# Two-layer latent transformer kernel: query work moved ahead, dequantisation shared out differently, and several pieces of work reordered

## The chip, the cores and the metric

The kernel runs on one core of a Trainium2 chip. A core has five engines that run at the same time, each through its own instruction list in order: PE (TensorE, matrix products), DVE (VectorE), ACT (ScalarE), POOL (GpSimd) and SP (SyncE, which here only starts DMA transfers). They meet through semaphores. The metric is the device time of one execution in microseconds (us). PE's clock has two levels in the records, 2.4 GHz (granted clock 1.00) and 1.2 GHz (0.50); a stretch that has both shows a value between.

## The reference

Sixteen samples of 64 latent rows (1024 rows of 512, held as 8 tiles of 128) attend to contexts of 1601 rows of 256. With LN the layer norm and x the latent rows:

```
x = x + cross_attention0(LN(x), ctx)   # 16 heads of 32, projections Wq Wk Wv Wo with biases
x = x + state_space(LN(x))             # 16 heads, 64 states, masked decay matrix, gate, W_out, b_out
x = x + block_ffn(LN(x))               # 16 blocks of 128 hidden units, the best 4 by a router kept
x = x + cross_attention1(LN(x), ctx)   # one head: q = LN(x) Wq + bq, k = ctx Wk + bk, v = ctx Wv + bv
x = x + self_attention(LN(x))          # causal
x = x + quantised_ffn(LN(x))           # weights to 4 bits in groups of 32; activations to 16 bits,
                                       # each with one scale from the largest magnitude of the tensor
```

Weights of the last line are quantised so, with w in groups of 32 along a row:

```
s  = max(max|w| / 7, 1e-12)
wq = clip(round(w / s), -8, 7) * s
```

## The kernel before

The kernel is a chain of stages. Each stage is a block in which every engine has a hand-written instruction list, and all engines wait for each other between two blocks. The stages and their times in the profiled execution are: cross attention 0 (0 to 864.3 us), state space (to 1000.2), block FFN (to 1231.65), queries of cross attention 1 (to 1288.0), its batches (to 1434.8), self attention (to 1491.75) and quantised FFN (to 1747.1). Nothing but the written order decides when an instruction comes; there is no planner.

Precision is kept by splitting: an fp32 operand becomes a bf16 high part and a bf16 rest (low part), and three products are taken. Some stages use fp32 matmuls instead, which stand as two records each in the trace.

**Cross attention 0** (`cross0_batches`). At the start DVE makes the high and low halves of the queries (L835, L837), SP writes the queries to DRAM in another layout (L440) and reads them back (L419). POOL builds `picks`, a matrix that chooses heads, out of a memset and three selections on 128x2048 (L518, L521), SP stores it (`head_picks`, L436), and it is read again only in state space and block FFN. Then 16 samples of 8 head pairs follow: scores, softmax, transposes of the probabilities by DMA (L458, L463), products with the values (L621). `ring_events` deals PE's other work, the projections of the next sample (L588) and the outputs of the last (L639), between the pairs. After the last sample a drain remains: the last products, their sums by DVE (L805), the value bias (`folded`, L650), row sums (L657) and the last output tile (L639, L881). Meanwhile SP loads x again tile by tile (L473, in `X_BEHIND`), and `residual(t)` on DVE adds the finished outputs to it (L796) and takes its statistics (L79).

**State space** (`state_space`). After the projections DVE adds the output bias to all eight tiles of x (L1207), each counted by the semaphore `s_xo`. Then come 32 units (tile, group of heads): ACT exponentiates, DVE multiplies the decay matrix in (L1221) and gates (L1212), PE makes the products (L1105, L1127). POOL and SP use the stage to split the block FFN's weights: POOL first waits for all eight counts of `s_xo`, then takes sixteen pieces (high part L994, low part L996), SP loads each piece and stores its two parts (L1037). SP ends the stage with a wait for the last stores.

**Block FFN** (`block_ffn`). PE makes 32 hidden groups (12 matmuls L1366 and a mask L1371 each); ACT applies relu into `masked`, a ring of two buffers (L1421), and rounds the high part (L1410); POOL takes the low part (L1329). Then PE makes 8 output tiles of 48 matmuls (L1401), and DVE adds each to x (L1526). In the same stage `Dequant` quantises the last layer's weights in 36 pieces of 128x512: SP loads a piece, DVE takes the scales, divides and rounds (L2095, L2097, L2099, L2101, L2104, L2106), POOL multiplies by the scale (L2111), ACT rounds the high part (L2118), DVE takes the low part (L2122), SP turns both parts by DMA (L2068) and stores them (L2074). `front_at` and `turn_at` give the slot of each piece: 16 turns fall to hidden groups, 20 come behind them, three pieces to an output tile.

**Queries of cross attention 1** (`cross1_queries`). Scores of one head need q.k = (x Wq + bq).(c Wk + bk), so the kernel turns Wk onto the query side: qT = Wq'x + bq in 8 groups of 4 fp32 matmuls (L1601), a row bk.qT (L1607), and qk = Wk qT in 4 groups (L1614). SP loads the weights, then the first four samples' contexts (13.1 MB). All is PE work behind a layer norm and transposes (L219).

**Quantised FFN** (`quant_ffn`). PE runs 24 gate groups and 24 up groups of 12 matmuls (L2219), then the down product (L2235). DVE takes largest magnitudes (L2341, L2364, L2398), reduces them over the tile (`peak_of`, L2303), has PE spread them over partitions (`spread`, L2204) and computes scales (`unit`). The scale number 2, of the gated values, is found in front of the last up group: `spread(2)` stands before the last 12 matmuls.

## Time and profile before

| what | us |
|---|---|
| median of 3 runs | 1748.54 |
| lowest and highest | 1747.14, 1748.58 |
| the profiled execution | 1748.78 |
| its span (first to last instruction) | 1747.1 |
| PE busy | 1586.8 (91%) |
| DVE busy | 1179.9 (68%) |
| ACT busy | 889.2 (51%) |
| POOL busy | 770.7 (44%) |

Busy shares are means over stages with different limits. Since the engines meet between stages, the time is the sum of the stages' lengths, and each stage ends with its own slowest engine. Where this is not PE, PE shows a gap with the engine it waited for, and behind a long gap its clock is at the lower level for a while. The rows to look for are therefore PE's gaps, the lower clock behind them, and at a stage's end the engines that waited there for the last one.

### The profile page before, as it was taken

What the parts mean: (1) busy time and instruction counts of PE and PEld (TensorE: products, weight loads), DVE (VectorE), ACT (ScalarE), POOL (GpSimd) and SP (SyncE); (2) the same over time, 40 slices, a digit from 0 to 9 for tenths busy, and PEclk for the clock granted to TensorE, in tenths of its full rate; (3) what the DMA queues carried; (4) which work ended last, traced back from release to release, by engine and by line L of the source; (5) the groups of instructions that cost most, each with busy time, mean ns of one, the idle gap of its engine ahead of it and who ended that gap; (6) DMA issues with size and microseconds to landing.
All of it is one profiled execution on the core that took longest, in us unless ns stands there. A gap on an engine that the chain in (4) does not pass through costs nothing. (4 is left out here: it accounts for less than half of the span.)

```text
span 1747.1 us, 33847 instructions
## 1 busy us (share of the span) xinstructions
PE 1586.8 (91%) x13876; PEld 812.5 (47%) x13876; DVE 1179.9 (68%) x1959; ACT 889.2 (51%) x1184; POOL 770.7 (44%) x384
## 2 busy tenths in 40 slices
PE   6999999999999999999589899799789979799459
PEld 3445555555555555554346463244434444344224
DVE  6688888888888888886555468988422223527881
ACT  1377777778777777776273035411111222327650
POOL 1468888888888878875108516633000000000000
PEclk9999999999999999999699979999899999899879
DMA  4489999999999999999617454567838944000001
GB/s 143 115 162 197 192 189 193 193 191 191 198 191 191 192 193 195 192 174 175 141 50 223 149 217 124 145 157 175 338 128 342 397 160 208 0 1 1 0 0 48
DMA packets 556821, 282.72 MB, mean 162 GB/s; under 512 B 483056, under 2 KB 534768, under 8 KB 553600
## 3 DMA queue, kind: packets, MB, share of 16 engines
q1 hardware_dynamic: 556672, 280.63, 67.7%
q8 instruction: 106, 1.74, 0.4%
q14 instruction: 43, 0.35, 0.1%
HBM read 138.74 MB, written 22.54 MB: 92 GB/s over the span
## 5 line engine op out<-in xcount | busy, mean ns | idle before, releaser
L564 POOL TENSOR_TENSOR x<-x_prob,x 128x1604 bf16<-128x1604 f32 x120 | 387.9, 3233 | 144.7 <-ACT x L720 144.7
L850 DVE TENSOR_REDUCE x_negmax<-x_score 128x1 f32<-128x1604 f32 x128 | 233.6, 1825 | 17.7 <-PE x_score L605 7.4
L588 PE MATMUL x_ring<-x_ctx_hi,wk_split 128*128 128x400 bf16 (+1 forms) x1024 | 218.3, 335 | 4.4 <-DVE x_kT L778 4.4
L710 ACT ACTIVATE x_prob<-x_score,x_negmax 128x1604 f32<-128x1604 f32 x128 | 204.8, 1600 | 25.7 <-DVE x_negmax L850 20.9
L588 PE MATMUL x_ring<-wv_split,x_ctx_hi 128*128 128x512 bf16 (+1 forms) x832 | 214.2, 380 | 0.0
L778 DVE SCALAR_TENSOR_TENSOR x_kT<-x_ring,bk,x_kT 128x400 bf16<-128x400 f32 (+1 forms) x256 | 162.0, 634 | 34.6 <-ACT x_kT L699 26.6
L720 ACT CAST x<-x_prob 128x1604 bf16<-128x1604 f32 x120 | 183.0, 1525 | 0.0
L784 DVE TENSOR_TENSOR x_v<-x_ring,x_v 128x512 bf16<-128x512 f32 (+1 forms) x208 | 143.7, 691 | 52.8 <-ACT x_v L703 50.0
L699 ACT ACTIVATE x_kT<-x_ring,bk 128x400 bf16<-128x400 f32 (+1 forms) x196 | 116.4, 594 | 98.0 <-PE x_ring L588 97.0
L588 PEld LDWEIGHTS x_ring<-x_ctx_hi,wk_split 128*128 128x128 bf16 x1024 | 94.4, 97 | 92.4 <-issue 21.1
L703 ACT CAST x_v<-x_ring 128x512 bf16<-128x512 f32 (+1 forms) x148 | 86.5, 585 | 97.2 <-PE x_ring L588 97.2
L2219 PE MATMUL g_bank<-g_x_split,g_w 128*128 128x512 bf16 x576 | 129.0, 388 | 6.4 <-DVE g_x_split L2335 6.4
L621 PE MATMUL x_pv<-x_pT,x_v 128*64 128x128 bf16 (+1 forms) x3328 | 119.0, 222 | 13.0 <-DMA x_pT<-x_kT 5.7
L588 PE MATMUL x_ring<-x_ctx_lo,wk_split 128*128 128x400 bf16 (+1 forms) x512 | 129.3, 334 | 0.0
L621 PEld LDWEIGHTS x_pv<-x_pT,x_v 128*64 128x64 bf16 (+1 forms) x3328 | 98.2, 111 | 64.2 <-issue 58.7
L588 PEld LDWEIGHTS x_ring<-wv_split,x_ctx_hi 128*128 128x128 bf16 (+1 forms) x832 | 77.4, 99 | 102.3 <-DVE x_kT L778 9.2
L588 PE MATMUL x_ring<-wv_split,x_ctx_lo 128*128 128x512 bf16 (+1 forms) x416 | 123.7, 379 | 0.0
L2196 POOL MEMSET g_round<- 128x1 f32 x1 | 0.1, 98 | 272.5 <-POOLq L1845 272.5
L513 POOL TENSOR_TENSOR x_ctx_lo<-x_stage,x_ctx_hi 128x802 bf16<-128x802 f32 (+1 forms) x64 | 106.1, 1658 | 29.6 <-DVE x_ctx_hi L759 28.3
L1401 PE MATMUL f_bank<-f_w,f_h 128*128 128x512 bf16 x384 | 85.4, 385 | 16.2 <-POOL f_h L1329 13.8
L506 POOL TENSOR_TENSOR x_ctx_hi<-x_stage,x_zero 128x800 bf16<-128x800 f32 (+1 forms) x60 | 91.3, 1521 | 9.6 <-DMA x_stage<-in_ctxT 7.7
L2219 PEld LDWEIGHTS g_bank<-g_x_split,g_w 128*128 128x128 bf16 x576 | 57.5, 100 | 77.2 <-DVE g_x_split L2335 6.6
(332 smaller groups left out, 2491.2 us busy)
## 6 DMA issues: line engine op xcount, KB each, us to landing
y_ctx<-in_ctx SPq DMA_DIRECT2D x16, 1664.0 KB, 10.5
y_ctxT<-in_ctxT SPq DMA_DIRECT2D x16, 1601.0 KB, 13.6
x_stage<-in_ctxT SPq DMA_DIRECT2D x48, 400.0 KB, 4.5
x_q_rows<-q_rows SPq DMA_DIRECT2D x64, 128.0 KB, 3.1
m_xT<-in_L_ffn_w SPq DMA_DIRECT2D x16, 512.0 KB, 4.6
ffn_w_parts<-m_xT SPq DMA_DIRECT2D x32, 256.0 KB, 2.6
x_stage<-in_ctxT SPq DMA_DIRECT2D x16, 401.0 KB, 5.0
f_w<-ffn_w_parts SPq DMA_DIRECT2D x4, 1024.0 KB, 9.1
```

The costliest lines, as they stand in the source:

```text
L506: pool.tensor_tensor(chi[:, :, QW * c:QW * c + n], stage[:, c % 2, :, 0:n], zero[:].unsqueeze(2).broadcast_to([P, KC, n]), ALU.add).then_i ...
L513: pool.tensor_tensor(clo[:, :, at], stage[:, c % 2, :, 0:n], chi[:, :, at], ALU.subtract).then_inc(clo_done, 1)
L564: pool.tensor_tensor(ph[:, g % 2, 1, 0:NKP], prob[:, g % 2, :], ph[:, g % 2, 0, 0:NKP], ALU.subtract).then_inc(pl_done, 1)
L588: last = pe.matmul(out_, lhs, rhs, start=(i == 0), stop=(i == len(steps) - 1))
L621: last = pe.matmul(pv[L * h:L * h + L, 0:2 * L], v[0:kw, vpar, t, 2 * pp + h, :, :].rearrange("p s d -> p (s d)"), pT[0:kw, u, :, t, L * h ...
L699: nc.scalar.activation(kT[:, par, 0, m, n0:n0 + w], ring[g % RING][:, 0:w], ACT.Identity, bias=bk[:, KD * turned(c) + m:KD * turned(c) + m ...
L710: nc.scalar.activation(prob[:, g % 2, :].rearrange("p (c n) -> p c n", n=QW), scores, ACT.Exp, bias=nmax[:, g % 2:g % 2 + 1], accum_out=rs ...
L720: nc.scalar.copy(ph_of[g >= LAST][:, g % 2, 0, 0:NKP], prob[:, g % 2, :]).then_inc(ph_done, 1)
L778: dve.scalar_tensor_tensor(kT[:, par, 1, m, n0:n0 + w], ring[g % RING][:, 0:w], bk[:, KD * turned(c) + m:KD * turned(c) + m + 1], kT[:, pa ...
L784: dve.tensor_tensor(v[0:kw, par, m, :, 1, :], ring[g % RING][0:kw, :].rearrange("p (h d) -> p h d", h=H), v[0:kw, par, m, :, 0, :], ALU.su ...
L850: dve.tensor_reduce(nmax[:, pair % 2:pair % 2 + 1], scores, mybir.AxisListType.XY, ALU.max, negate=True).then_inc(max_done, 1)
L2219: last = pe.matmul(banks[2 + n % NB_G][:], wt[:, hw, j, m * P:(m + 1) * P], xs[:, hx, j, 512 * c:512 * c + 512], start=(i == 0 and j == 0) ...
```

## The change

1. *Start.* On POOL the four memsets of the `ph` padding (L542, which wait for the stored queries) come ahead of `picks` and its three selections; on SP the store of `picks` and the wait for it move behind the store of the queries, their reads, four chunk loads and the load of `Wo`. PE gets 18 matmuls on an identity matrix ahead of its first transposes.
2. *Drain.* The loads of x tiles 6 and 7 move from behind pair 6 of the last sample to behind pair 7, with a semaphore of their own; `residual` is called for tiles (0,1,2), (3), (4) and, after the last output piece, (5,6,7), where it was (0 to 3), (4,5), (6,7). PE gets 20 such matmuls before the last pair's products, 8 before and 8 after the folded bias.
3. *State space.* The eight bias adds move into the unit loop, one behind `mixed(n)` of units 4 to 11.
4. *Block FFN.* The ring `masked` has three buffers. The multiplication by the scale goes from POOL to DVE, the low part from DVE to POOL. Behind the turn of piece 23 SP loads Wq transposed, [Wk transposed | bk] and bq into the space of w1 (1.5 MB), and behind the last output tile PE makes the product Wq.[Wk'|bk] from them (16 fp32 matmuls of 257 columns, 12 of one column); ACT copies it out.
5. *Queries of cross attention 1.* qT is gone: qk comes from x in 4 groups of 4 matmuls with the product, and 8 matmuls make the bias row. Four weight loads are gone, the context loads go sample pair by sample pair, and DVE adds the folded query bias.
6. *Self attention and quantised FFN.* 15 identity matmuls at the start of each; in the latter 18 more behind the transposes and 12 before the down product. Scale 2 is found behind the last up group, the 15 steps of the gate chain are spread over 12 tiles instead of 11, and `AHEAD` goes from 3 to 1.

```diff
+    def keep_busy(self, pe, ident, bank, count):
+        pattern = ident[:].bitcast(BF16)
+        for _ in range(count):
+            pe.matmul(bank[:, 0:2 * P], pattern[:, 0:P], pattern, start=True, stop=True)
...
-        X_BEHIND = {2: (0,), 3: (1, 2), 4: (3,), 5: (4, 5), 6: (6, 7)}
+        X_BEHIND = {2: (0,), 3: (1, 2), 4: (3,), 5: (4, 5), 7: (6, 7)}
+        X_EARLY = 6
...
-            sp.wait_ge(s_pick, 4)
-            sp.dma_start(k.picks, picks.rearrange("p h n -> p (h n)")).then_inc(s_kept, 16)
-            sp.wait_ge(s_kept, 16)
             sp.wait_ge(s_qlo, len(qgroups))
...
             for c in range(4):
                 low_part(0, c)
+            pool.wait_ge(spilled, 64)
+            for u in range(2):
+                for h in range(2):
+                    pool.memset(ph_of[0][:, u, h, NKP:NKT], 0.0).then_inc(set_ph, 1)
             pool.memset(picks, 0.0).then_inc(s_pick, 1)
...
+            pe.wait_ge(norm.s_stats, 5)
+            k.keep_busy(pe, ident, ring[0], 18)
             norm.on_tensor(pe)
...
+                            if e[1] == PAIRS - 1:
+                                pe.wait_ge(exp_done, PAIRS)
+                                k.keep_busy(pe, ident, score[:, 0:512], 20)
                             products(e[1])
...
-                    if b == B and p < 2:
-                        for t in ((0, 1, 2, 3), (4, 5))[p]:
+                    if b == B and p < 3:
+                        for t in ((0, 1, 2), (3,), (4,))[p]:
                             residual(t)
...
-            for t in range(NT):
-                dve.tensor_tensor(x[:, t, :], x[:, t, :], bO[:], ALU.add).then_inc(s_xo, 1)
...
                 mixed(n)
+                if 4 <= n < 4 + NT:
+                    dve.tensor_tensor(x[:, n - 4, :], x[:, n - 4, :], bO[:], ALU.add).then_inc(s_xo, 1)
...
+MASKED = 3
...
+            def late_weights():
+                sp.wait_ge(s_h, len(groups))
+                sp.dma_start(bq[:], d["L1_xattn_bq"]).then_inc(s_late, 16)
+                sp.dma_start(wqT, d["L1_xattn_WqT"].rearrange("(j p) n -> p j n", p=P)).then_inc(s_late, 16)
+                sp.dma_start(wkb, d["L1_xattn_WkTb"].rearrange("(j p) n -> p j n", p=P)).then_inc(s_late, 16)
...
-                for i in dq.fronts(n):
-                    dq.multiply_on_gpsimd(pool, i)
-            for i in range(dq.EARLY, dq.count):
-                dq.multiply_on_gpsimd(pool, i)
+                for i in dq.turns(n):
+                    dq.low_on_gpsimd(pool, i)
...
+            pe.wait_ge(s_late, 48)
+            for a in range(KD):
+                for j in range(KD):
+                    last = pe.matmul(banks[2 + a][:, 0:CD + 1], wqT[:, j, a * P:(a + 1) * P], wkb[:, j, :],
+                                     start=(j == 0), stop=(j == KD - 1))
+                last.then_inc(s_next, 1)
...
-                if n >= 2:
-                    act.wait_ge(s_hlo, n - 1)
+                if n >= MASKED:
+                    act.wait_ge(s_hlo, n - MASKED + 1)
...
-                for i in dq.turns(n):
-                    dq.low_on_vector(dve, i)
...
-                    last = pe.matmul(wide[n % 3][:], wq[:, j, m * P:(m + 1) * P],
+                    last = pe.matmul(keyed[n][:], wqk[:, j, m * P:(m + 1) * P],
                                      xT[:, j, 512 * c:512 * c + 512], start=(j == 0), stop=(j == KD - 1))
...
-        if i >= self.SLOTS:
-            dve.wait_ge(self.s_back, i - self.SLOTS + 1)
...
+        dve.wait_ge(self.s_unit, 6 * i + 6)
+        dve.tensor_tensor(blocks, blocks, s.unsqueeze(2).broadcast_to([P, 512 // QB, QB]),
+                          ALU.mult).then_inc(self.s_back, 1)
...
-                if n == half + 2 * FIRST:
-                    spread(2)
+            spread(2)
             spread(3)
             spread(4)
+            k.keep_busy(pe, ident, banks[1], 12)
```

At the start of the kernel, POOL's list around `picks` (named x_pT here, the padding x 128x60) reads before:

```order
L518 MEMSET x_pT 128x2048
L521 AFFINE_SELECT x_pT<-x_pT 128x2048 x3
L523 MEMSET tri 128x128
L524 MEMSET low 128x128
L527 AFFINE_SELECT tri<-tri 128x128
L531 AFFINE_SELECT tri<-tri 128x64
L534 AFFINE_SELECT low<-low 128x128
L537 AFFINE_SELECT low<-low 128x64
L542 MEMSET x 128x60 x4
```

and now:

```order
L529 MEMSET x 128x60 x4
L530 MEMSET x_pT 128x2048
L533 AFFINE_SELECT x_pT<-x_pT 128x2048 x3
L535 MEMSET tri 128x128
L536 MEMSET low 128x128
L539 AFFINE_SELECT tri<-tri 128x128
```

The padding, which waits for the stored queries, now stands ahead of all of them.

In state space, DVE's list between the gate projections (m_gT) and the units reads before (m_bO is the output bias):

```order
L1204 TENSOR_SCALAR m_gT<-m_banks,m_bG 128x512 x8
L1207 TENSOR_TENSOR x<-x,m_bO 128x512 x8
L1221 TENSOR_TENSOR m_mix<-m_decay,m_banks 128x2x128 x6
L1212 TENSOR_TENSOR m_xhat<-m_banks,m_gT 128x128
L1221 TENSOR_TENSOR m_mix<-m_decay,m_banks 128x2x128 x2
L1212 TENSOR_TENSOR m_xhat<-m_banks,m_gT 128x128
```

and now:

```order
L1221 TENSOR_SCALAR m_gT<-m_banks,m_bG 128x512 x8
L1236 TENSOR_TENSOR m_mix<-m_decay,m_banks 128x2x128 x6
L1227 TENSOR_TENSOR m_xhat<-m_banks,m_gT 128x128
L1236 TENSOR_TENSOR m_mix<-m_decay,m_banks 128x2x128 x2
L1227 TENSOR_TENSOR m_xhat<-m_banks,m_gT 128x128
L1236 TENSOR_TENSOR m_mix<-m_decay,m_banks 128x2x128 x2
L1246 TENSOR_TENSOR x<-x,m_bO 128x512
L1227 TENSOR_TENSOR m_xhat<-m_banks,m_gT 128x128
L1236 TENSOR_TENSOR m_mix<-m_decay,m_banks 128x2x128 x2
L1246 TENSOR_TENSOR x<-x,m_bO 128x512
```

One add stands behind each unit from the fifth on, so the eighth count of `s_xo` comes with the twelfth unit.

From the block FFN's output tiles (f_h) to the first scores of cross attention 1, PE's list reads before:

```order
L1401 MATMUL f_bank<-f_w,f_h 128x512 x384
L1254 UNCONDITIONAL_BRANCH
L1589 UNCONDITIONAL_BRANCH
L219 MATMUL yq_bank<-ident,yq_xhat 128x128 x32
L1601 MATMUL yq_bank<-yq_xT,yq_wq 128x512 x32
L1607 MATMUL yq_bank<-yq_qT,yq_bk 1x512 x8
L1614 MATMUL yq_bank<-yq_qT,yq_wkT 128x512 x16
```

and now:

```order
L1436 MATMUL f_bank<-f_w,f_h 128x512 x384
L1442 MATMUL f_bank<-f_w 128x257 x16
L1447 MATMUL f_bank<-f_next_bq,f_w 128x1 x8
L1450 MATMUL f_bank<-f_next_bq,f_w 1x1 x4
L1274 UNCONDITIONAL_BRANCH
L1628 UNCONDITIONAL_BRANCH
L225 MATMUL yq_bank<-ident,yq_xhat 128x128 x32
L1635 MATMUL yq_bank<-yq_xT,wqk 128x512 x12
L1641 MATMUL yq_bank<-yq_xT,wqk 1x512 x8
L1635 MATMUL yq_bank<-yq_xT,wqk 128x512 x4
```

The 32 matmuls of the query projection are gone from the second stage, and 28 small ones have come to the end of the first (an empty branch marks the passage between stages).

## Rows read from the trace of the kernel before

**Rows 1.** Timeline of DVE, start: start us, us, line, op, out<-in, [idle before <-releaser]

```profile
44.20 0.69 DVE L837 TENSOR_TENSOR x<-x_prob,x 128x512 bf16<-128x512 f32 x1
...
49.17 2.39 DVE L837 TENSOR_TENSOR x<-x_prob,x 128x512 bf16<-128x512 f32 x1
```

**Rows 2.** Timeline of POOL, start

```profile
49.01 6.56 POOL L521 TENSOR_SCALAR_AFFINE_SELECT x_pT<-x_pT 128x2048 bf16<-128x2048 bf16 x3
```

**Rows 3.** Timeline of PE, start

```profile
56.96 1.52 PE L588 MATMUL x_ring<-x_ctx_hi,wk_split 128*128 128x401 bf16 x4 [4.12 <-DVE x_kT L778]
```

**Rows 4.** Stretch: us, busy of PE PEld DVE ACT POOL, PEclk, DMA share, GB/s

```profile
56.00:62.00 6.00, 5.04 (x16) 2.29 (x17) 2.71 (x9) 1.19 (x2) 0.99 (x4) 0.50 0.67 189
```

**Rows 5.** Timeline of PE, drain of cross attention 0

```profile
833.44 3.70 PE L639 MATMUL x_ring<-wo,catT 128*128 128x512 f32 x8
...
843.47 1.59 PE L621 MATMUL x_pv<-x_pT,x_v 128*64 128x128 bf16 x26 [5.48 <-DMA x_pT<-x_kT]
850.36 1.60 PE L621 MATMUL x_pv<-x_pT,x_v 128*64 128x128 bf16 x26 [5.29 <-DVE x_kT L805]
...
856.34 6.11 PE L639 MATMUL x_ring<-wo,catT 128*128 128x512 f32 x8 [1.01 <-DVE catT L866]
```

**Rows 6.** Timeline of DVE in state space

```profile
910.79 4.89 DVE L1207 TENSOR_TENSOR x<-x,m_bO 128x512 f32<-128x512 f32 x8
...
919.34 0.75 DVE L1221 TENSOR_TENSOR m_mix<-m_decay,m_banks 128x256 f32<-128x256 f32 x2 [0.81 <-PE m_banks L1127]
```

**Rows 7.** Timeline of PE in state space

```profile
916.40 0.43 PE L1105 MATMUL m_banks<-m_mix,m_xn 128*32 128x128 f32 x8 [1.79 <-DVE m_mix L1221]
```

**Rows 8.** Timeline of POOL in state space, its first and last piece

```profile
916.19 1.89 POOL L994 TENSOR_TENSOR m_xT<-m_xT,m_zero_col 128x1024 bf16<-128x1024 f32 x1 [51.22 <-DMA m_xT<-in_L_ffn_w]
...
985.70 2.13 POOL L996 TENSOR_TENSOR m_xT<-m_xT 128x1024 bf16<-128x1024 f32 x1
```

**Rows 9.** Waits of SP at the end of state space: us in total, times, longest

```profile
SPq L904 <- PEq L904: 10.0, 1, 10.0
```

**Rows 10.** Waits of ACT, 1020 to 1140 us

```profile
ACT f_masked L1421 <- POOL f_h L1329: 29.1, 29, 1.3
```

**Rows 11.** Timeline of PE, first output tile of block FFN

```profile
1136.95 13.21 PE L1401 MATMUL f_bank<-f_w,f_h 128*128 128x512 bf16 x51 [13.77 <-POOL f_h L1329]
```

**Rows 12.** Groups of instructions, 1020 to 1232 us: busy us, mean ns | idle before

```profile
L2111 POOL TENSOR_TENSOR f_stage<-f_stage,w_scale 128x512 f32<-128x512 f32 x36 | 51.6, 1433 | 69.8 <-DVE f_stage L2106 69.8
...
L2101 DVE TENSOR_TENSOR f_stage<-f_stage,w_scale 128x512 f32<-128x512 f32 x36 | 33.1, 918 | 1.2
L2122 DVE TENSOR_TENSOR w_parts<-f_stage,w_parts 128x512 bf16<-128x512 f32 x36 | 32.6, 908 | 6.7 <-ACT w_parts L2118 6.6
```

**Rows 13.** Timeline around the end of block FFN

```profile
1224.89 0.69 DVE L1526 TENSOR_TENSOR x<-x,f_bank 128x512 f32<-128x512 f32 x1 [2.97 <-PE f_bank L1401]
...
1231.65 1.28 ACT L174 ACT_TABLE_LOAD   x1 [11.78 <-PEq L88]
```

**Rows 14.** Timeline of PE in the query stage of cross attention 1

```profile
1240.97 27.63 PE L1601 MATMUL yq_bank<-yq_xT,yq_wq 128*128 128x512 f32 x64
1269.45 3.60 PE L1607 MATMUL yq_bank<-yq_qT,yq_bk 128*1 128x512 f32 x16 [0.84 <-DVE yq_qT L1630]
1272.98 14.00 PE L1614 MATMUL yq_bank<-yq_qT,yq_wkT 128*128 128x512 f32 x32
```

**Rows 15.** Stretches of the query stage and the quantised FFN (columns as in rows 4)

```profile
1240.00:1270.00 30.00, 29.16 (x78) 13.13 (x78) 12.10 (x18) 0.65 (x2) 0.00 (x0) 1.00 1.01 426
...
1505.00:1510.00 5.00, 2.69 (x7) 1.04 (x8) 4.83 (x11) 2.56 (x4) 0.00 (x0) 0.50 0.00 0
...
1680.00:1685.00 5.00, 5.00 (x16) 1.89 (x15) 4.89 (x6) 5.00 (x6) 0.00 (x0) 0.62 0.00 0
```

**Rows 16.** Timeline of the quantised FFN at its last up group

```profile
1636.40 0.48 PE L2204 MATMUL g_bank<-ident,g_peak 128*128 128x128 f32 x1 [4.20 <-DVE g_peak L2303]
```

223 lines of the change are left out of this document (117 added, 106 removed).

## The prediction

> **What bounds the kernel now.** I read three views in turn: the waits and gaps of PE in the timeline, stage by stage, since all engines meet between stages; behind each long gap the granted clock of the stretch; and at a stage's end who waited for whom. PE is busy 91% of the span, so what can be won is the work that PE need not do there, its gaps, and the time at the lower clock behind them. Seven places are touched. At the start PE waits 4.12 us for DVE and then works at 0.50 [rows 3, 4]. In the drain it waits 5.48 us for a transposed piece and 5.29 us for DVE, and the last output tile takes 6.11 us where the one before took 3.70 us [rows 5]. State space ends with PE and DVE, and SP has waited 10.0 us by then [rows 9]. Block FFN's output tiles start 13.77 us late, behind POOL, whose low parts ACT waited for 29 times [rows 10, 11]. The query stage is nearly all PE: 27.63, 3.60 and 14.00 us [rows 14]. The quantised FFN starts its gate half and its down half at a low clock [rows 15], and its last up group waits 4.20 us for DVE [rows 16].
>
> **The change part by part.** The sum is made against the profiled execution, 1748.78 us, 0.24 us over the median.
>
> *Start.* DVE's low part of the queries takes 0.69 us alone and 2.39 us beside POOL's selections of 6.56 us [rows 1, 2]. Two of these and the two casts ahead of them lose about 5.9 us together, more than PE's gap of 4.12 us. The selections now wait for the stored queries, so POOL is idle there; the gap goes. The stretch behind it has 5.04 us of PE work at 0.50 [rows 4], half of it is saved: 2.5. Sum -6.6 us. Cover: on SP the store of `picks` passes the query store, the reads and four chunk loads, all of which come earlier for it, and it is read in state space only. POOL's 8.4 us of selections now stand ahead of the next sample's splits, but these also start some 6 us earlier; if that cover fails, PE waits at most about 2 us for a split. The 18 identity matmuls cost between +0.5 and -0.5; I take 0.
>
> *Drain.* SP no longer puts two loads in front of the last pair's transposes, and DVE has three tiles, not four, ahead of the sum that PE waited for [rows 5]. But the 20 matmuls that now stand before the last products take some 4 us from 845.1 on (256 columns at half clock, by the row of 6.11 us for 4096 columns at mostly half clock about 0.2 each), so these products start at about 849.3 instead of 850.36: -1.1. Warm, they save 0.7 and the output tile 2.4 (6.11 to 3.70), the small matmuls between some 0.7, DVE's shorter list 0.6. Sum -5.5 us; bounds -2 (the clock doesn't hold) and -7.
>
> *State space.* The first add block of 4.89 us [rows 6] leaves the path, but PE's gap behind it is only 1.79 us [rows 7]; the units come 1.8 us earlier. They take 1.764 us each (30 rows of L1221, the first of them in [rows 6]), and DVE is idle 0.81 us in each, which hides an add of 0.61 us. What follows is the cost: POOL waits for all eight adds, and the eighth stands behind the twelfth unit, 915.8 + 9 x 1.764 + 0.75 + 0.6 = 933.0, where POOL started at 916.19 [rows 8]: 16.8 us later. Its sixteen pieces are a chain of loads, splits and stores (69.5 us + 2.1, first to last row) that no other engine shortens. SP was done 10.0 us ahead of the others [rows 9], who now finish 1.8 us earlier. So the stage ends 16.8 - 10.0 = +6.8 us later, with the store's landing about +7.0. Bounds: +5 if the chain runs tighter, +8. This is a term against the change. It would be -1.8 if POOL weren't held.
>
> *Block FFN.* DVE's low part (908 ns) is exchanged for a product like that of L2101 (918 ns) [rows 12], so DVE's sum per piece, about 3.95 us, stays. What changes is who waits: POOL's multiplication stood in its list between the hidden groups' low parts and waited for DVE, with it ACT and the masked ring; DVE was busy without a pause over the last 80 us of the groups and ran late. Now the piece's low part comes two slots behind its front, and DVE need not wait for ACT (6.6 us, [rows 12]). The last hidden group ends at 1123.2; relu, rounding and low part behind it take 0.69 + 0.61 + 1.24, so the output tiles start at about 1126, not 1136.95 [rows 11]: -10.7. After it the tiles go at the pace of DVE and SP (three pieces each, 13.0 us a tile), which I take as unchanged. The last tile is added at 1214.5 instead of 1224.89 [rows 13]. Then PE makes the product for the next stage: 32 records of 257 columns, half of the 0.4375 us that one of 512 takes [rows 14], 7.0 us, and 2.6 us for the small ones, 0.7 us for the last copy. The stage, which ended at 1231.65 on SP's last stores [rows 13], ends at about 1225.5, by PE: -6.0 us. The loads of 1.5 MB take SP 1.5 us and the DMA some 3.6 us at the 426 GB/s of [rows 15]; they come in the middle of the tiles and may delay one piece. Bounds: -10 and +2.
>
> Here a rule speaks against the exchange. The row first: L2122 is 0.7 us alone and up to 1.68 us beside POOL, its mean 908 ns, and the start shows the same [rows 1, 12]. The Trainium skill says in "SBUF — State Buffer", section "Who interferes with whom", that a VectorE instruction with two SBUF inputs shuts out a GpSimd instruction that reads SBUF and the other way round, and "Perfetto Trace Analysis", section "Optimizing Scalar/DVE Operations", warns that moving work between the two may not help. By that rule the swap is neutral, since both sides had two inputs before, and the term stays as it is.
>
> *Query stage.* 27.63 us and the 0.84 us wait behind it go [rows 14]; the 3.60 and the 14.00 us stay in kind (the same 8 and 16 matmuls). DMA was at 426 GB/s through the first 30 us with weights and contexts [rows 15]; 2.5 MB fewer are loaded, and the first two contexts need 6.5 MB, 15 us, inside a stage of 28 us; the second pair is wanted later. -28.4 us; bounds -26 and -29.
>
> *Self attention, quantised FFN.* Warm starts: each of the stretches behind an idle start has 2.7 to 5 us of matmuls at 0.50 to 0.68 [rows 15]. I take -1.0 for self attention, -2.5 for the gate half (14.9 us for 55 matmuls, which warm take 11.9), -1.5 for the down half. The late peak: the last 12 up matmuls no longer wait 4.20 us [rows 16], but DVE's list is as long, so only the last group's rest comes forward: -1.6, bounds -3 and +1.5.
>
> Sum: -6.6 - 5.5 + 7.0 - 6.0 - 28.4 - 1.0 - 2.5 - 1.6 - 1.5 = -46.1, and 1748.8 - 46.1 = 1702.7 in such an execution, 1702.5 as a median.
>
> **The rivals.**
> 1. *POOL's delay in state space stays hidden.* For it: the last loads and stores could run closer. Against it: the pieces followed each other at 4.3 us without a long gap, and 16.8 is more than 10.0 + 1.8. It would give -1.8 instead of +7.0: 1693.7.
> 2. *The output tiles don't start earlier,* because DVE is late with piece 15, which ACT must round before the last two groups, or the tiles go slower. For it: DVE had no pause before. Against it: it can now run ahead, a piece each 4.8 us in the list against 3.95 us of work. The stage then ends at 1224.9 + 9.6 + 0.7 = 1235 instead of 1231.65, +3.5 and not -6.0: 1712.
> 3. *The identity matmuls don't hold the clock.* Then their time is added in the drain (4 us against the 1.1, 2.4 and 0.7 taken) and the starts give nothing: +9.5: 1712.
> 4. *Slower than before: the weight pieces.* If GpSimd and VectorE shut each other out in turn, each of the 20 pieces behind the groups could cost more than the 4.3 us of now. All engines one after the other make 3.95 + 0.62 (ACT) + 1.43 [rows 12] and some 0.3 between them, 6.3 us a piece, +40 over 20 pieces; the earlier start of the tiles is gone (+6), and late loads in such a chain cost some 5: 1702.5 + 51 = 1753.5. It is slower than before by over 0.2% from 1.95 us more per piece on. Against it: the pieces are in four slots, so that the engines overlap, as the trace shows now.
> 5. *The query work isn't saved,* because the contexts' DMA sets the stage's end: 13.1 MB at 426 GB/s are 31 us, against the 28 of the stage. It would cost 3 to 5 us: 1706, inside the range.
>
> **How the numbers follow.** Forecast with its small deviations 0.55, rival 1 0.12, rival 2 0.13, rival 3 0.10, rival 4 0.02, rival 5 0.08. The bounds of the terms together reach about 9 us to either side. 1692 takes in rival 1, 1715 rivals 2 and 3 with some deviation; the two together, 1721, are left out. A measurement of this kernel can tell 0.2%, 3.5 us. All cases but the fourth are faster by far more: faster 0.97, within 0.2% 0.015, slower 0.015.
>
> **What would show it.** Start: no gap of PE before the second set of projections, clock 1.00 behind it. Drain: the last products at about 849, the last output tile in 3.7 us. State space: POOL's first piece at about 926 in the new time (933 less 6.6), DVE and PE waiting 8 to 9 us for SP at the stage's end. Block FFN: first output tile less than 4 us behind the last mask, the last work by PE. Query stage 28 us long. If POOL's pieces start where they did, the third term is wrong; if the tiles start 13 us behind the masks, the fourth; if the stage of queries lasts over 31 us, its DMA is the bound. The whole is wrong if a stage outside the seven places changes its length, above all the batches of cross attention 1, which take over a shorter lead of loads.

## The result and the profile after

The changed kernel takes 1725.12 us (median of 4 runs, 1724.09 to 1726.45); the kernel before takes 1748.47 us (median of 4, 1747.14 to 1748.58). The ratio is 0.9869, 95% interval 0.9852 to 0.9886. That is a gain of 23.4 us, half of the 46.1 forecast, and outside the range of 1692 to 1715. The profiled execution has a span of 1724.7 us.

The head of the page of the changed kernel: busy time, and TensorE's clock in 40 slices of 43 us.

```profile
span 1724.7 us, 33914 instructions
PE 1559.3 (90%) x13873; PEld 813.5 (47%) x13982; DVE 1188.4 (69%) x1951; ACT 889.0 (52%) x1190; POOL 765.6 (44%) x384
...
PEclk9999999999999999999899969989899999999779
```

PE is still the busiest engine, and at nearly full clock but for a few slices. Where the time went shows only by stage. A stage ends where SP issues the next one's first loads; the last stage has none there and begins with its engines' first instructions. Lengths in us, of one profiled execution each:

| stage | before | after | change | forecast |
|---|---|---|---|---|
| cross attention 0 (start and drain) | 864.31 | 851.12 | -13.2 | -12.1 |
| state space | 135.89 | 141.72 | +5.8 | +7.0 |
| block FFN | 231.45 | 242.88 | +11.4 | -6.0 |
| query stage | 56.34 | 27.63 | -28.7 | -28.4 |
| batches of cross attention 1 | 146.86 | 151.16 | +4.3 | 0 |
| self attention | 56.90 | 59.26 | +2.4 | -1.0 |
| quantised FFN | 255.35 | 250.93 | -4.4 | -5.6 |

The changes sum to -22.4. Four rows came as forecast within 1.2 us. Three did not: block FFN is off by 17.4 us, the batches by 4.3, self attention by 3.4. A stage with unchanged code differs from one profiled execution to the next, most in cross attention 0; where that bears on a reading, the spread is given with it.

**Block FFN.** The timeline of PE at its first output tile, in the changed kernel, answers [rows 11]:

```profile
1115.30 0.39 PE L1406 MATMUL f_bank<-f_maskT,f_sel 16*128 16x512 bf16 x1
1134.94 10.28 PE L1436 MATMUL f_bank<-f_w,f_h 128*128 128x512 bf16 x40 [19.25 <-POOL f_h L1363]
```

The hidden groups end as far into the stage as before (122.8 us after its start, before 123.0). But PE then waits 19.25 us, where it waited 13.77 and about 3 were forecast. The waits of the stage, 1012 to 1235 us (in total, times, longest), tell who is late; the last one answers [rows 10]:

```profile
ACT w_parts L2154 <- DVE f_stage L2147: 111.1, 31, 4.3
POOL f_h L1363 <- ACT f_h L1459: 78.8, 23, 38.5
...
ACT f_masked L1470 <- POOL f_h L1363: 0.2, 1, 0.2
```

ACT no longer waits for POOL's low parts: the third masked buffer does what it should. ACT waits for DVE instead, 31 times, and since it works in order, the last hidden groups' values wait behind a weight piece. PE's last mask ends at 1115.69; ACT then still takes three pieces between hidden groups (the first at 1117.88), and POOL's last low part releases PE's first output tile:

```profile
1123.99 0.62 ACT L2154 CAST w_parts<-f_stage 128x512 bf16<-128x512 f32 x1 [3.30 <-DVE f_stage L2147]
...
1129.27 0.62 ACT L2154 CAST w_parts<-f_stage 128x512 bf16<-128x512 f32 x1 [3.56 <-DVE f_stage L2147]
1129.79 0.68 ACT L1470 ACTIVATE f_masked<-f_bank,f_b 128x512 f32<-128x512 f32 x1
```

```profile
1133.47 1.33 POOL L1363 TENSOR_TENSOR f_h<-f_masked,f_h 128x512 bf16<-128x512 f32 x1
```

Why is DVE late? Its groups of instructions over 1012 to 1236 us (busy, mean ns of one) answer [rows 12]:

```profile
L2140 DVE TENSOR_TENSOR f_stage<-f_stage,w_scale 128x512 f32<-128x512 f32 x36 | 36.3, 1007 | 1.2
...
L2147 DVE TENSOR_TENSOR f_stage<-f_stage,w_scale 128x512 f32<-128x512 f32 x36 | 33.4, 929 | 1.2
L2143 DVE TENSOR_SCALAR f_stage<-f_stage 128x512 f32<-128x512 f32 x36 | 27.6, 768 | 1.2
...
L2145 DVE TENSOR_SCALAR f_stage<-f_stage 128x512 f32<-128x512 f32 x36 | 23.9, 663 | 1.2
```

The new product (L2147) costs 929 ns, as forecast. It is above all the two rounding instructions, which the diff doesn't touch, that grew: from means of 426 and 497 ns to 768 and 663. One piece from DVE's timeline shows it, first in the kernel before:

```profile
1083.36 0.69 DVE L2101 TENSOR_TENSOR f_stage<-f_stage,w_scale 128x512 f32<-128x512 f32 x1
1084.09 0.43 DVE L2104 TENSOR_SCALAR f_stage<-f_stage 128x512 f32<-128x512 f32 x1
1084.55 1.26 DVE L2106 TENSOR_SCALAR f_stage<-f_stage 128x512 f32<-128x512 f32 x1
```

POOL in that kernel stands idle for part of the time, first for ACT, then for DVE's rounding:

```profile
1084.37 1.15 POOL L1329 TENSOR_TENSOR f_h<-f_masked,f_h 128x512 bf16<-128x512 f32 x1 [1.36 <-ACT f_h L1410]
1085.89 1.43 POOL L2111 TENSOR_TENSOR f_stage<-f_stage,w_scale 128x512 f32<-128x512 f32 x1 [0.36 <-DVE f_stage L2106]
```

The same piece in the changed kernel, DVE and then POOL:

```profile
1075.42 0.69 DVE L2140 TENSOR_TENSOR f_stage<-f_stage,w_scale 128x512 f32<-128x512 f32 x1
1076.15 1.26 DVE L2143 TENSOR_SCALAR f_stage<-f_stage 128x512 f32<-128x512 f32 x1
1077.45 1.27 DVE L2145 TENSOR_SCALAR f_stage<-f_stage 128x512 f32<-128x512 f32 x1
1078.75 1.53 DVE L2147 TENSOR_TENSOR f_stage<-f_stage,w_scale 128x512 f32<-128x512 f32 x1
```

```profile
1075.52 1.61 POOL L1363 TENSOR_TENSOR f_h<-f_masked,f_h 128x512 bf16<-128x512 f32 x1 [2.37 <-ACT f_h L1459]
1077.09 1.33 POOL L2158 TENSOR_TENSOR w_parts<-f_stage,w_parts 128x512 bf16<-128x512 f32 x1
1078.39 1.33 POOL L1363 TENSOR_TENSOR f_h<-f_masked,f_h 128x512 bf16<-128x512 f32 x1
```

A rounding takes 0.43 us unless a POOL instruction is under way when it starts; then it takes 1.26 to 1.41 us and ends 0.28 or 0.29 us behind that instruction. In the changed kernel this holds without exception: 24 of the 72 roundings start beside a running POOL instruction and are slow, the other 48 take 0.43 us. In the kernel before only 3 of 72 are slow. There POOL's multiplication could not begin until the piece's roundings were done; now POOL's three subtractions can come back to back, and both roundings may lie beside them.

All slow ones are among the first 17 pieces, which lie beside the hidden groups. The mean over 36 pieces hides this: over these 17, DVE's instructions for a piece take 4.49 us before and 5.47 now. The list has one such piece for each 4.8 us (17 pieces over 27 groups of 3.01 us). DVE was behind it before as well, one piece in 5.5 us in the mean, and is further behind now, one in 5.9: the 17th piece starts 129.4 us into the stage before and 136.3 now, and the output tiles follow.

**State space.** POOL's first piece and DVE at the stage's end answer [rows 8]:

```profile
919.69 1.89 POOL L1011 TENSOR_TENSOR m_xT<-m_xT,m_zero_col 128x1024 bf16<-128x1024 f32 x1 [67.90 <-DVE x L1246]
```

```profile
992.88 0.73 DVE L138 BATCH_NORM_AGGREGATE f_meanvar<-x_stats 128x2 f32<-128x6 f32 x8 [8.21 <-PEq L921]
```

SP, which waited 10.0 us for the others [rows 9], now waits 0.2, and DVE waits 8.21 us for it. In five more kernels with this edit the stage takes 142.3 to 143.7 us, so 141.7 is the low end.

**Batches and self attention.** DVE in the first batch, then PE in the first products of self attention:

```profile
1274.85 0.16 DVE L1852 TENSOR_TENSOR y_stat<-y_stat,y_cqs 128x1 f32<-128x1 f32 x1 [3.97 <-DMA y_cqs<-y_cq]
```

```profile
1417.76 2.90 PE L225 MATMUL s_bank<-ident,sn_xhat 128*128 128x128 f32 x24 [1.42 <-DVE sn_xhat L157]
1422.88 5.40 PE L1928 MATMUL s_bank<-s_xT,s_wq 128*128 128x512 f32 x8 [2.21 <-DMA s_wv<-in_L_attn_Wv]
```

The stretches around that wait (columns as in [rows 4]; the clock is the third number from the end):

```profile
1420.00:1423.00 3.00, 0.79 (x8) 0.55 (x6) 1.47 (x3) 1.19 (x3) 0.00 (x0) 1.00 1.12 459
1423.00:1426.00 3.00, 3.00 (x6) 1.25 (x7) 0.00 (x0) 0.00 (x0) 0.00 (x0) 0.71 1.01 434
```

A load of a few numbers (y_cqs) was issued behind the contexts and waited for: DMA moves 412 GB/s in 1263 to 1273 us. In self attention the warmed transposes end early, PE waits 2.21 us for a weight, and the eight products behind that wait take 5.40 us: the granted clock, still 1.00 (2.4 GHz) up to the wait, is 0.71 in the mean behind it, so part of the stretch runs at the lower level of 1.2 GHz. That fall does not come each time. The kernel of the first experiment below (e1) has the same code in this stage and waits as long, and its products take 3.70 us:

```profile
1414.77 3.70 PE L1931 MATMUL s_bank<-s_xT,s_wq 128*128 128x512 f32 x8 [2.26 <-DMA s_wv<-in_L_attn_Wv]
```

Of the six profiled kernels with these identity matmuls, four show 5.40 us behind waits of 1.93 to 2.21 us (the stage then takes 58.9 to 59.3 us), and two show 3.70 behind 2.26 and 1.49 (57.6 and 56.8).

### The profile page after: what moved, and what is told of

Same layout as the page of the kernel before. It is cut to its first block and busy times, and to the rows that moved or that the text cites. A ratio compares the mean times of both kernels' runs of the same rounds, so it can differ in the third digit from the quotient of the medians.

```text
span 1724.7 us, 33914 instructions
## 1 busy us (share of the span) xinstructions
PE 1559.3 (90%) x13873; PEld 813.5 (47%) x13982; DVE 1188.4 (69%) x1951; ACT 889.0 (52%) x1190; POOL 765.6 (44%) x384
## 5 line engine op out<-in xcount | busy, mean ns | idle before, releaser
L596 PE MATMUL x_ring<-wv_split,x_ctx_hi 128*128 128x512 bf16 (+1 forms) x770 | 200.3, 379 | 9.6 <-issue 7.1
L801 DVE TENSOR_TENSOR x_v<-x_ring,x_v 128x512 bf16<-128x512 f32 (+1 forms) x208 | 143.7, 691 | 52.8 <-ACT x_v L720 50.0
L716 ACT ACTIVATE x_kT<-x_ring,bk 128x400 bf16<-128x400 f32 (+1 forms) x196 | 116.4, 594 | 91.1 <-PE x_ring L596 90.1
L596 PEld LDWEIGHTS x_ring<-x_ctx_hi,wk_split 128*128 128x128 bf16 x1024 | 93.9, 97 | 86.9 <-issue 19.7
L2257 PE MATMUL g_bank<-g_x_split,g_w 128*128 128x512 bf16 x564 | 125.1, 382 | 2.0 <-DVE g_x_split L2373 1.4
L613 PE MATMUL x_score<-x_kT,x_q_rows 32*64 32x400 bf16 (+1 forms) x3072 | 91.6, 336 | 0.7 <-ACT x_prob L727 0.7
## 6 DMA issues: line engine op xcount, KB each, us to landing
y_ctx<-in_ctx SPq DMA_DIRECT2D x16, 1664.0 KB, 10.5
```

Source lines behind the costliest of these rows:

```text
L596: last = pe.matmul(out_, lhs, rhs, start=(i == 0), stop=(i == len(steps) - 1))
L613: last = pe.matmul(score[L * u:L * u + L, 512 * c:512 * c + w], qp[rows, par, a, hq, p // 2, :], kT[rows, par, hk, p // 2, QW * c:QW * c + w],
L716: nc.scalar.activation(kT[:, par, 0, m, n0:n0 + w], ring[g % RING][:, 0:w], ACT.Identity, bias=bk[:, KD * turned(c) + m:KD * turned(c) + m ...
L801: dve.tensor_tensor(v[0:kw, par, m, :, 1, :], ring[g % RING][0:kw, :].rearrange("p (h d) -> p h d", h=H), v[0:kw, par, m, :, 0, :], ALU.su ...
L2257: last = pe.matmul(banks[2 + n % NB_G][:], wt[:, hw, j, m * P:(m + 1) * P], xs[:, hx, j, 512 * c:512 * c + 512], start=(i == 0 and j == 0) ...
```

## The experiments

Each edit is against the changed kernel unless the text says otherwise. Times are medians, ratios are to the kernel before; lengths of stages are of one profiled execution each. "Tile start" is the first output tile of block FFN, counted from the stage's start: 136.8 us before, 142.1 after.

**The exchange taken back (e1).** POOL multiplies and VectorE takes the low part again.

```diff
-                for i in dq.turns(n):
-                    dq.low_on_gpsimd(pool, i)
+                for i in dq.fronts(n):
+                    dq.multiply_on_gpsimd(pool, i)
...
+                for i in dq.turns(n):
+                    dq.low_on_vector(dve, i)
...
-        dve.tensor_tensor(blocks, blocks, s.unsqueeze(2).broadcast_to([P, 512 // QB, QB]),
-                          ALU.mult).then_inc(self.s_back, 1)
```

> The changed kernel with the old division of the dequantisation (the multiplication by the scale on POOL, the low part on DVE); the ring of three buffers and the moved product stay. Theory: the new division makes DVE's two rounding instructions meet POOL's instructions (their means rose from 0.43 and 0.50 us to 0.77 and 0.66), DVE falls behind, and ACT, which stands in order behind DVE's pieces, holds back the last hidden groups. Then the gap of PE ahead of the first output tile falls from 19.3 us to 14 or less, the rounding instructions are back at 0.43 and 0.50, block FFN takes 236 to 238 us instead of 242.9, and the total is about 1719.5. Rival: the late start comes from the order of the lists alone; then gap and total stay (1725).

Measured: 1716.14 us, ratio 0.9821 (0.9792 to 0.9850). Block FFN lasts 234.9 us instead of 242.9, tile start 132.3. The rounding instructions in this kernel, 1010 to 1228 us:

```profile
L2150 DVE TENSOR_SCALAR f_stage<-f_stage 128x512 f32<-128x512 f32 x36 | 17.9, 496 | 1.2
L2148 DVE TENSOR_SCALAR f_stage<-f_stage 128x512 f32<-128x512 f32 x36 | 17.0, 473 | 1.2
```

So the exchange itself costs 8.0 us beside the ring of three and the moved product, and with it gone the roundings are fast again: 5 of 72 are slow, and the 17th piece starts at 125.1.

**The exchange alone (e5),** in the kernel before, with its ring of two and nothing else of the change.

```diff
-                for i in dq.fronts(n):
-                    dq.multiply_on_gpsimd(pool, i)
+                for i in dq.turns(n):
+                    dq.low_on_gpsimd(pool, i)
```

> The kernel before with only the new division of the dequantisation (multiplication by the scale on DVE, low part on POOL, the wait on it gone); the ring keeps two buffers. Theory: the division costs by itself, since DVE's rounding instructions now meet POOL's: their means rise from 0.43 and 0.50 to about 0.77 and 0.66 us, PE's gap ahead of the output tiles rises from 13.8 to 19 us or more, block FFN takes 236 to 240 us instead of 231.5, total 1752 to 1757. Rival (the prediction's): DVE's work per piece is the same and POOL no longer waits in the middle, so the output tiles start up to 10 us earlier and the total is 1740 to 1747.

Measured: 1753.14 us, ratio 1.0029 (1.0016 to 1.0041): alone, it makes the kernel slower. Block FFN is 4.5 us longer than before, tile start 144.1, and PE waits 20.96 us ahead of the tiles. The roundings take 748 and 704 ns in the mean, 25 of 72 are slow, and the tiles start 7.3 us later; 3.8 us of this come back at the stage's end, where SP's last stores take 3.0 us behind the last add instead of 6.8. State space, whose code is unchanged, is 3.2 us longer in this profile, because of PE's clock: from 50 us into the stage on, behind the 1.79 us wait of [rows 7], two stretches of 5 us show granted clocks of 0.72 and 0.60, where the kernel before shows 1.00 in both behind the same wait. The exchange has no part in that.

**The third masked buffer alone (e8),** in the kernel before.

```diff
-        masked = k.sb(ctx, "f_masked", [P, 2, 512])
+        masked = k.sb(ctx, "f_masked", [P, MASKED, 512])
...
-                if n >= 2:
-                    act.wait_ge(s_hlo, n - 1)
+                if n >= MASKED:
+                    act.wait_ge(s_hlo, n - MASKED + 1)
```

> The kernel before with only the third buffer in the masked ring of block FFN. Theory: in the kernel before, ACT waited 29 times for POOL's low part; the third buffer takes these waits away and PE's gap ahead of the output tiles falls from 13.8 to about 9.7 us, as with the old division in the changed kernel. Block FFN 227.5 us instead of 231.5, total 1744.5. Rival: DVE holds the chain and the gap stays at 13.8 us; no change.

Measured: 1742.83 us, ratio 0.9972 (0.9955 to 0.9990). Block FFN is 5.3 us shorter, tile start 132.2; ACT's 29 waits of 29.1 us are gone. PE still waits 9.73 us for the last hidden value, as in e1 (9.75):

```profile
1132.58 12.71 PE L1404 MATMUL f_bank<-f_w,f_h 128*128 128x512 bf16 x46 [9.73 <-POOL f_h L1332]
```

From the kernel before to the changed one the stage thus takes three steps: -5.3 (e8), +8.7 for the product at the stage's tail (e1 over e8) and +8.0 for the exchange (changed kernel over e1). They sum to the whole by construction, so that is no check of them; with the ring of two the exchange cost 4.5 (e5). The tail's 8.7 has two halves. From the last tile's add to the end it is 10.7 us, where SP's stores took 6.8. And from the first tile to the last add it takes 91.9 us in e1, 87.2 in e8: in e1, DVE waits 9.1 us for pieces' loads (5.6 the longest), in e8 4.3 (1.1 the longest). That the late weights, which the tiles' DMA carries besides, cause these waits is not shown: the next kernel (e6) loads them too, and its tiles take 85.7 us with 1.2 us of such waits.

**POOL's new work cut short (e6).**

```diff
-        pool.tensor_tensor(self.parts[:, i % self.PARTS, 1, :], self.w[:, i % self.SLOTS, :],
-                           self.parts[:, i % self.PARTS, 0, :], ALU.subtract).then_inc(self.s_lo, 1)
+        pool.tensor_tensor(self.parts[:, i % self.PARTS, 1, 0:32], self.w[:, i % self.SLOTS, 0:32],
+                           self.parts[:, i % self.PARTS, 0, 0:32], ALU.subtract).then_inc(self.s_lo, 1)
```

> The changed kernel in which POOL takes the low part of a weight piece for the first 32 of 512 columns only (the rest stays zero, so the last layer's weights lose their low parts); order and waits are unchanged. Theory: DVE is slow because POOL's instructions run beside it. With POOL's reduced to a fraction, the two rounding instructions fall from 0.77 and 0.66 us towards 0.5, PE's gap ahead of the output tiles falls from 19.3 us to below 12, and block FFN gets 5 us shorter or more. Rival: the order of the lists holds ACT; then durations may fall, but the gap stays above 16 us.

Measured: 1704.21 us (one run). Block FFN lasts 223.9 us, 19.0 less than with the full subtraction; tile start 127.5, PE's wait there:

```profile
1120.65 9.64 PE L1438 MATMUL f_bank<-f_w,f_h 128*128 128x512 bf16 x32 [5.33 <-POOL f_h L1365]
```

DVE's instructions are the same as in the changed kernel, and the two products fell from 1007 and 929 ns to 767 and 859, the roundings from 768 and 663 to 574 and 476. What POOL does at the time sets DVE's pace: 8 of 72 roundings are slow. POOL's list is shorter here too, so the 19.0 us are not the price of the contention alone. Even so the tiles start 1.7 us behind the forecast's 125.8.

**The low part two slots later (e7).**

```diff
-        return self.front_at(i) + 2
+        return self.front_at(i) + 4
```

> The changed kernel with a piece's turn (ACT's high part, POOL's low part) four slots behind its front on DVE, not two. Theory: ACT's list, in which the high part of a piece stands between the hidden groups, carries DVE's delay over to the hidden groups. With more room the gap of PE ahead of the output tiles falls from 19.3 to about 10 us although DVE's rounding instructions stay at 0.6 to 0.8 us, block FFN takes about 234 us, total 1717. Rival: DVE's backlog grows to more than four slots (12 us), or the later turns delay the loads of the next pieces as much, and the gap stays.

Measured: 1722.69 us, ratio 0.9862 (0.9841 to 0.9882). The tiles start at 137.3 instead of 142.1, as a theory of late ACT has it, with 15.1 us of wait where I expected 10. But then they take 94.4 us instead of 90.1, with 7.6 us of waits for DVE, and DVE waits 6.7 us for a piece's load: the stage ends where it did (242.5 us, where I expected 234). The roundings still take 667 and 665 ns. This way of moving the delay gains nothing.

**The adds ahead of the units again (e2).**

```diff
+            for t in range(NT):
+                dve.tensor_tensor(x[:, t, :], x[:, t, :], bO[:], ALU.add).then_inc(s_xo, 1)
```

(and the add inside the unit loop gone)

> The changed kernel with the eight bias adds ahead of the 32 units again. Theory: the stage ended on POOL's and SP's weight pieces, which waited for the eighth add; state space falls from 141.7 to about 136 us, and PE and DVE no longer wait for SP at its end; total 1719.3. Rival: the stage is longer for another reason (the adds inside the units lengthen them); then the units' period of 1.764 us must be longer in the changed kernel, and the gain would be the same 6 us without SP being late.

Measured: 1718.72 us, ratio 0.9825 (0.9794 to 0.9855). State space is back at 135.84 us; POOL's first piece:

```profile
902.38 1.89 POOL L1011 TENSOR_TENSOR m_xT<-m_xT,m_zero_col 128x1024 bf16<-128x1024 f32 x1 [50.80 <-DVE x L1224]
```

17.1 us earlier into the stage, and 5.9 us come back, by the same arithmetic as the forecast's third term. Moving the adds was a pure loss of 5.9 us.

**The second pair's contexts behind the first batch's loads (e3).**

```diff
-                for s in range(2):
+                for s in range(2 if u == 0 else 0):
...
+            for s in range(2):
+                sp.dma_start(cn[:, 1, s].rearrange("p t c -> p (t c)"), d["ctx"][2 + s]).then_inc(cn_in[1], 16)
```

> The changed kernel with the second sample pair's contexts in rows (3.4 MB) loaded in the next stage, behind the small loads of the key bias of the queries. Theory: in the changed kernel this small load stood behind 13.1 MB that the shorter query stage no longer covered, and DVE waited 3.97 us for it. It lands at once, the batches take 147 us instead of 151.2, total 1721. Rival: the batches are longer because they lack the lead of loads; then they stay at 151 us or get longer, since one load starts later still.

Measured: 1721.32 us, ratio 0.9846 (0.9816 to 0.9876). The 3.97 us wait is gone from the row. The batches last 148.7 us here, where I expected 147, and 146.9 to 147.0 in the four kernels below that have the same edit. That is before's 146.9, so up to all of the 4.3 us; e8, with before's code in this stage, shows 148.1.

**No identity matmuls at the start and in self attention (e4).**

```diff
-            pe.wait_ge(norm.s_stats, 5)
-            k.keep_busy(pe, ident, ring[0], 18)
...
-            k.keep_busy(pe, ident, banks[7], 15)
```

> The changed kernel without the 18 identity matmuls at the start of the kernel and without the 15 at the start of self attention. Theory: at the start they delay PE's first transposes by 1.1 us and give nothing; in self attention PE comes to its projections before their weights have landed (2.21 us), and its clock falls in the wait, so that the projections take 5.40 us instead of 3.67. Without them: start -1.1, self attention 57 us instead of 59.3, total 1721.7. Rival: the weights themselves land later than before and the clock would fall anyway; then self attention stays at about 59 us.

Measured: 1725.65 us, ratio 0.9875 (0.9840 to 0.9911). Self attention gives 2.1 us back (57.2):

```profile
1419.26 4.29 PE L225 MATMUL s_bank<-ident,sn_xhat 128*128 128x128 f32 x24 [4.99 <-DVE sn_xhat L157]
1424.00 3.70 PE L1926 MATMUL s_bank<-s_xT,s_wq 128*128 128x512 f32 x8 [0.46 <-DMA s_wv<-in_L_attn_Wv]
```

The transposes are slower by 1.4 us, end just before the weight is there, and the clock holds for the products. The 2.1 us are thus the price of the clock's fall, which e1 and e6 escape with the identity matmuls in place. At the start I had expected 1 us to come back, and a total of 1721.7; neither came. Cross attention 0 varied between 847.7 and 852.8 us over the profiles, and its first products come at 98.0 to 100.0 us with the same start, at 98.9 and 99.0 without the 18 matmuls. So single profiles say nothing there below 2 us.

**The four findings together (e9):** e1, e2, e3 and the self-attention part of e4.

> The changed kernel with four parts taken back or mended together: the old division of the dequantisation, the bias adds ahead of the units, the second pair's context rows loaded in the batches' stage, no identity matmuls at the start of self attention. Theory: the four act in different stages and add up: -8.0 in block FFN, -5.9 in state space, -2.5 in the batches, -2.0 in self attention, 1725.1 - 18.4 = 1706.7. Rival: they share a resource across the stages (the later loads), and the sum falls short by 3 us or more.

Measured: **1703.04 us, ratio 0.9749 (0.9732 to 0.9767),** the fastest kernel of this study and 22.1 us below the changed one, where I expected 18.4. The stages: 847.7, 135.8, 235.4, 27.6, 146.9, 57.0, 248.6. The two profiled executions are 25.8 us apart: the four parts give 20.0 us in their own stages, and cross attention 0 (-3.5) and the quantised FFN (-2.4), which have the same code in both, vary by that much.

**Without the other identity matmuls (e10),** against e9: those of the drain and of the quantised FFN gone, those of the start kept.

```diff
-                            if e[1] == PAIRS - 1:
-                                pe.wait_ge(exp_done, PAIRS)
-                                k.keep_busy(pe, ident, score[:, 0:512], 20)
...
-            pe.wait_ge(norm.s_xT, 1)
-            k.keep_busy(pe, ident, banks[0], 18)
...
-            k.keep_busy(pe, ident, banks[1], 12)
```

> The kernel with the four parts taken back or mended (e9_four_back) without the identity matmuls of the drain (20, 8, 8) and of the quantised FFN (15, 18, 12). Theory: they hold the clock. Without them the last output tile of the drain takes 6.1 us and the stage 847.7 + 1.5 to 3 us (the 20 also delay the last products by some 2 us, which comes back), the gate half starts 2 us colder and the down half 1.7; quantised FFN 252 us instead of 248.6, total about 1709. Rival: they give nothing (clock and lengths stay as they are): 1703.

Measured: 1710.38 us, ratio 0.9785 (0.9746 to 0.9825). The quantised FFN is 5.4 us longer (253.9); its expected length was 252. The drain, from the third-last products to the stage's end, is 19.7 us; with these matmuls it is 19.4 in e9 and 19.4 to 21.2 in the nine profiled kernels that have them. The last output tile takes 3.70 us without them, not 6.1.

**Without those of start and drain (e13),** against e9.

```diff
-            pe.wait_ge(norm.s_stats, 5)
-            k.keep_busy(pe, ident, ring[0], 18)
...
-                            if e[1] == PAIRS - 1:
-                                pe.wait_ge(exp_done, PAIRS)
-                                k.keep_busy(pe, ident, score[:, 0:512], 20)
```

> The kernel e9_four_back (1703.0 us) without the identity matmuls of the first stage, at its start (18) and in its drain (20, 8, 8); those of the quantised FFN stay. Theory: they give nothing there. Without the 20, the last products come as soon as their transposes have landed, some 3 us earlier, and the two effects of a cold clock cancel that; from the third last products on the drain takes 19.4 to 20.5 us, with or without them, and the rest of the stage differs by about 1 us from run to run: 1702 to 1705. Quantised FFN stays at 248.6 to 249.6 us, against 253.9 without its own. Rival: they hold the clock in the drain, and the drain gets 2 us longer or more.

Measured: 1706.76 us, ratio 0.9762 (0.9738 to 0.9785). The drain takes 20.3 us, which lies among the kernels with them. The total is above the 1702 to 1705 that I expected; its interval and that of e9 overlap. Cross attention 0 takes 852.1 us, in e9 847.7, and most of that lies ahead of the drain: from the first products to the third-last it is 732.9 us here and 733.4 in e4, the two changed kernels without the 18 matmuls at the start, against 730.2 to 731.6 in the nine that have them. Nothing in between differs among them. PE's waits for transposed pieces there sum to 3.0 and 3.8 us, in e9 to 1.1. Whether the 18 matmuls have to do with it, these single profiles do not show; that they are worth some 2 us stays possible. PE's timeline of this drain, and then that of the changed kernel:

```profile
838.26 1.60 PE L629 MATMUL x_pv<-x_pT,x_v 128*64 128x128 bf16 x26 [5.54 <-DMA x_pT<-x_kT]
841.44 1.60 PE L629 MATMUL x_pv<-x_pT,x_v 128*64 128x128 bf16 x26 [1.58 <-DMA x_pT<-x_kT]
...
846.54 3.70 PE L647 MATMUL x_ring<-wo,catT 128*128 128x512 f32 x8 [1.02 <-DVE catT L874]
```

```profile
836.74 1.24 PE L629 MATMUL x_pv<-x_pT,x_v 128*64 128x128 bf16 x26 [4.60 <-DMA x_pT<-x_kT]
837.91 3.65 PE L88 MATMUL x_score<-ident 128*128 128x256 bf16 x20
841.49 0.92 PE L629 MATMUL x_pv<-x_pT,x_v 128*64 128x128 bf16 x26
...
845.56 3.70 PE L647 MATMUL x_ring<-wo,catT 128*128 128x512 f32 x8
```

With the loads and adds out of the way the last products wait 1.58 us instead of 5.29 [rows 5], and the last output tile takes 3.70 us with or without the identity matmuls. In the drain these save 0.7 us on the products and take 3.65 us in front of them.

**The product ahead of the output tiles (e12),** against e9: into PE's idle gap, its weights called for eight pieces earlier.

```diff
-            dq.on_sync(sp, dq.EARLY + 6, late_weights)
+            dq.on_sync(sp, dq.EARLY - 2, late_weights)
```

(and PE's part on the product moved in front of the tiles)

> The kernel e9_four_back with the product for the next stage made in PE's gap between the hidden groups and the output tiles; its weights are loaded right behind the last hidden group. Theory: at the stage's end the product stands alone on PE for 9.5 us; in the gap of some 9.7 us about 4 us of it lie beside the wait for POOL's last low parts, and PE stays warm. Block FFN 231 us instead of 235.4, total 1699. Rival: loads and product start so late in the gap that the tiles are delayed by the whole product: no change, 1703.

Measured: 1713.33 us, ratio 0.9801 (0.9773 to 0.9829), 10.3 us slower than e9; my expectation fell.

```profile
1106.42 0.39 PE L1405 MATMUL f_bank<-f_maskT,f_sel 16*128 16x512 bf16 x1
1126.03 10.06 PE L1432 MATMUL f_bank<-f_w 128*128 128x257 f32 x32 [19.23 <-DMA f_w<-in_L_xattn_WkTb]
```

SP's issue of that load in the same kernel:

```profile
1118.05 0.53 SPq L1348 DMA_DIRECT2D f_w<-in_L_xattn_WkTb  x1
```

SP issues the late loads in order behind a piece's transposes, which wait for the pieces: at 1118.05, 11.2 us after the last hidden group, and the data is there 8 us later. The gap is there, but the weights for it are not; and behind a wait of 19 us the product takes 10.06 us, not 7.12.

## Why the prediction was wrong by half, and what of it was right

**Start: right. Drain: the sum nearly right, by luck.** At the start DVE's low part takes 0.69 us throughout, PE runs on without a gap, and the third-last products begin 5.9 us earlier (forecast 6.6 for the start). In the drain, from there on, 27.2 us became 19.9, -7.3 against -5.5 and a bound of -7. PE at the start of the changed kernel, and its stretch, answer [rows 3, 4]:

```profile
50.74 0.84 PE L596 MATMUL x_ring<-x_ctx_hi,wk_split 128*128 128x401 bf16 x4
```

```profile
56.00:62.00 6.00, 5.95 (x33) 3.09 (x32) 3.54 (x6) 3.28 (x6) 0.00 (x0) 1.00 0.96 221
```

The forecast's -5.5 for the drain was mostly credited to the identity matmuls (2.4 + 0.7 + 0.7). They give nothing within what the runs can tell: the reordering alone gives -6.9 (27.2 to 20.3 in e13). So the split was wrong, and two errors nearly cancelled: I had not seen that with shorter waits the last tile would be back at 3.70 us by itself (e10, e13), nor that the last products' wait would fall by 3.7 us. The working for the 20 matmuls was wrong too: 6.11 us for 4096 columns is 0.38 us for 256, not 0.2, and that row is of float32 matmuls, while these are bf16; they took 3.65 us, 0.18 each.

**State space: right in mechanism and size.** 16.8 us of delay less SP's 10.0 us of slack, and 0.2, was forecast as +7.0. The delay was 16.7 us into the stage, POOL's chain ran 1.0 us tighter (70.7 us instead of 71.6), +5.8 came, and e2 returns 5.9. Rival 1 falls. (The forecast's sign, POOL's first piece at 926, had left out what the drain gains; it came at 919.69.)

**Block FFN: the step that failed is "so DVE's sum per piece, about 3.95 us, stays".** It is 4.57 us: the means of the roundings grew by 0.34 and 0.17 us, that of the product ahead of them by 0.09 (918 to 1007 ns, [rows 12]). Over the first 17 pieces, which lie ahead of the tiles, it went from 4.49 to 5.47; my 3.95 was the mean over all 36. I priced the instructions that were exchanged and took the others as they were; yet POOL's work moved in time against them. A second step failed beside it, the path "relu, rounding and low part behind it take 0.69 + 0.61 + 1.24": it left out that ACT, in order, still owes weight pieces when the last group ends. From the last mask's end to the first tile it is 19.25 us in the changed kernel, 9.7 where the roundings are fast (e1, e8), and 5.3 with POOL's new work cut short (e6), nowhere the 2.5 of this sum. The tiles start 5.3 us later into the stage, not 10.7 earlier: 16.0 of the 17.4. The rest is the tiles, 90.1 us from the first matmul to the last add where I had 88.5. (Their pace is PE's, 10.5 us for the 48 matmuls of a tile, and not 13.0 us by DVE and SP as I wrote; the sum had used the length seen before, so this cost nothing.) Rival 2, DVE late with the pieces, is what happened, and I gave it 0.13; its evidence, no pause of DVE over the last 80 us, stood in my own text, and its price was still 8 us too low (+3.5 against +11.4), since it let the tiles start as before and not later. Rival 4 named the mechanism, that the two engines shut each other out, but looked for it in the pieces behind the groups, where from the 18th piece on no rounding is slow. The ring of three is good for -5.3 (e8), not -10.7.

The rule that I weighed was the right one, read too narrowly. The row shows a one-input rounding at 0.43 us beside an idle POOL and at 1.26 beside a working one. The Trainium skill says in "SBUF — State Buffer", section "Who interferes with whom", not only that instructions with two SBUF inputs contend with GpSimd, but that `tensor_scalar` can enter a mode in which it takes the port that both share, and that whoever issues first then blocks the other. The trace agrees: 24 of 24 roundings that start beside a running POOL instruction end 0.28 or 0.29 us behind it, and one that starts 0.18 us or more ahead of POOL's takes its 0.43. So two roundings in each piece had some 0.83 us to lose, by this case's rows; 24 of 72 lost it, against 3 before. e6 agrees too: 8 are slow there, each beside a full-width low part of POOL.

**Query stage: right.** 27.63 us long, 28.7 shorter. Rival 5's resource was the right one, in another stage: the contexts' DMA did not hold up the query stage, but a small load behind them held up the first batch by 4 us. The sum had no term for the batches; they cost 4.3 us. The prediction had said that a longer stage of batches would prove it wrong.

**Self attention: wrong in sign, +2.4 for -1.0.** I counted the clock's gain and not what PE meets when it comes sooner, a weight still on its way. Here the weight sets the time, warm transposes only lengthen the wait, and in this profile the clock fell in it. In e6 it did not, and the stage takes 56.8 us, before's 56.9: even then the -1.0 does not come.

**Quantised FFN: right, -4.4 against -5.6.** The identity matmuls give 5.4 us by e10 against e9 (forecast 4.0). The ten profiles with them and with the late peak show 248.6 to 251.0 us, e10 without them 253.9, so it is 3 to 5.4. Rival 3, that the identity matmuls don't hold the clock, is thus true of the drain and not of this stage. The rows of the changed kernel that answer [rows 15, 16]:

```profile
1485.74 2.55 PE L88 MATMUL g_bank<-ident 128*128 128x256 bf16 x11
1489.73 25.51 PE L2257 MATMUL g_bank<-g_x_split,g_w 128*128 128x512 bf16 x109 [1.44 <-DVE g_x_split L2373]
```

```profile
1654.75 2.77 PE L88 MATMUL g_bank<-ident 128*128 128x256 bf16 x12
1658.11 17.16 PE L2273 MATMUL g_bank<-g_wd,g_w 128*128 128x512 bf16 x73 [0.59 <-DVE g_w L2458]
```

Here the identity matmuls end 1.4 and 0.6 us before the work that they are for, and PE has to wait for nothing afterwards. The late peak is what e10 has left: 253.9 us against 255.4 before, -1.4 where -1.6 was forecast. By the stage's length alone this is not clear of noise: e8, with before's code there, takes 253.9 us too, since its clock rose sooner. The two make -6.8, as in e9. The changed kernel's own profiled execution shows 2.4 us less, with the same code as e9, and this again is the clock: 15.8 us into the stage, a stretch of 2.5 us at the first gate matmuls has a granted clock of 0.50 in the changed kernel and 1.00 in e9. The down half begins 1.6 us later into the stage and takes 0.8 us longer. So the same 18 identity matmuls bring the clock up sooner in one execution than in another.

## What to carry to other kernels

When work moves between two engines that slow each other, price every instruction that will lie beside the moved work, not only the moved one: here an exchange of equal operations cost 8 us, mostly through two instructions that nobody touched, because a wait that looked like waste had kept the engines apart (3 slow roundings with it, 24 without). And take the mean over the pieces that bind, not over all. Before moving small work off a path that has slack, ask who else waits for it (eight adds, 5.9 us), and look at the order in which small loads stand behind large ones. Filling PE's idle time with matmuls pays only if the real work then finds its data: it gave 3 to 5.4 us where it ended within 1.4 us of ready data, cost 2 in four profiles of six where a load came some 2 us later, and gave nothing that shows in the drain, where the clock was back for the last tile without it. A single profile is not enough for such a reading: with the same code and the same wait, the clock fell in one execution and not in the next.

## What of the hardware was not expected

- A rounding by VectorE (tensor_scalar, float32, 128x512) takes 0.43 us, and 1.26 to 1.41 if a GpSimd instruction is under way when it starts: 24 of 24 in the changed kernel, each ending 0.28 or 0.29 us behind the GpSimd instruction, and none of the other 48. A product of two such operands takes 0.69 us, and 1.53 in the piece shown above. At 1.26 and 1.53 the cheap instruction loses as much time as the dear one, about 0.83 us.
- Behind a wait of 2.21 us, and 2.9 us of warm transposes ahead of it, the granted clock fell to 0.71 (5.40 us for eight products instead of 3.70); behind 2.26 us in the same code of e1 it did not (3.70). In state space a wait of 1.79 us left the clock at 1.00 in the kernel before and at 0.72 in e5. And in the drain of e13 the clock was back for the last tile although PE had waited 5.5, 1.6, 0.4 and 1.0 us in the 14 us before it.
- A load of a few numbers issued behind megabytes of contexts landed some 4 us after DVE wanted it, with DMA at 412 GB/s; and loads placed in SP's list behind a piece's transposes were issued 11.2 us after the gap that they were meant for had begun.
